# Halved input to a grouped convolution, smaller tap products, and expert products in the order of the sums

## The reference, cut to what matters

```python
# 1. deformable convolution block on the group-normalised input (here one channel per group)
xn = gn(x)
x_proj = xn @ w_in + b_in
x1 = gelu(layernorm(depthwise_conv3x3(xn) + dw_b) * ln_g + ln_b)
offset = x1 @ w_off + b_off                      # 8 groups x 9 taps x 2
mask = softmax(x1 @ w_msk + b_msk over 9 taps)
out = sum over 9 taps of mask * bilinear_sample(pad(x_proj), position + tap + offset)
x = x + out @ w_out + b_out
# 2. attention over the 256 tokens of each image
t = x as tokens; n = layernorm(t)
t = t + softmax(n @ n.T) @ n
# 3. mixture of 8 experts, top 2
n = layernorm(t)
p = softmax(n @ router_w + router_b); top 2, renormalised
t = t + sum over the two chosen experts of p * (n @ expert_w[e] + expert_b[e])
```

## Time and profile before

| | |
|---|---|
| Median of 3 runs | 83.26 us (83.23 to 83.63) |
| Profiled execution, its own time | 83.83 us |
| Its span, first to last instruction | 82.1 us |
| TensorE busy, weight load busy | 70.6 us (86%), 58.5 us (71%) |
| VectorE, ScalarE, GpSimd busy | 54.7 us (67%), 42.8 us (52%), 48.4 us (59%) |
| Mean granted TensorE clock | 0.964 |

### The profile page before, as it was taken

The page is one execution under the profiler, slowest core; times in us unless marked ns, Lnnn a source line. Parts: engine busy times, 40 slices in busy tenths (PEclk is TensorE's granted clock), DMA queues, the critical chain, the costliest instruction groups (busy, mean ns, idle before and its releaser), DMA issues.

```text
span 82.1 us, 1760 instructions
## 1 busy us (share of the span) xinstructions
PE 70.6 (86%) x655; PEld 58.5 (71%) x655; DVE 54.7 (67%) x103; ACT 42.8 (52%) x141; POOL 48.4 (59%) x78
## 2 busy tenths in 40 slices
PE   1999999999599999899799999997797989999600
PEld 1989879867399988698799989775444767666200
DVE  1141530363996899999997996646235758999950
ACT  0353200499669256969994000365993430299910
POOL 5107089998599699999999997000003500248920
PEclk9999999999999999999999999999999999999555
DMA  0412182004870000000000000000000000000014
GB/s 0 131 43 57 26 168 28 10 8 140 241 198 0 8 4 0 0 0 4 0 0 8 4 0 0 0 0 8 0 0 0 0 0 8 0 0 0 0 33 95
DMA packets 5607, 2.51 MB, mean 31 GB/s; under 512 B 4623, under 2 KB 5135, under 8 KB 5599
## 3 DMA queue, kind: packets, MB, share of 16 engines
q1 hardware_dynamic: 4895, 2.14, 10.8%
q10 hardware_dynamic: 704, 0.26, 1.2%
HBM read 0.95 MB, written 0.26 MB: 15 GB/s over the span
## 4 chain that ended last, share of the span: by engine, by line
PE 26%; DVE 25%; ACT 5%; issue 3%; POOL 2%; POOLq 1%; DVEq 0%
PE ps L654 10%; DVE prod L313 6%; DVE image_all L1144 6%; DVE image_all L1346 4%; PE ps L643 4%; PE ps L775 3%; ACT image_all L1002 3%; POOL image_all L529 2%; PE ps L785 2%; PE ps L793 2%; PE ps L756 1%; DVE prod L1367 1%; PE ps L694 1%; PE ps L718 1%; PE ps L702 1%
## 5 line engine op out<-in xcount | busy, mean ns | idle before, releaser
L538 PE MATMUL ps<-wide_ident 128*128 128x128 f32 x104 | 15.8, 309 | 1.8 <-POOL wide_ident L396 1.8
L538 PEld LDWEIGHTS ps<-wide_ident 128*128 128x128 f32 x104 | 14.3, 218 | 3.2 <-POOL wide_ident L396 1.8
L1144 DVE TENSOR_TENSOR image_all<-ps,images 128x896 f32<-128x896 f32 (+4 forms) x8 | 13.2, 1690 | 0.4 <-PE ps L643 0.4
L654 PE MATMUL ps<-wide_ident,image_all 128*128 128x128 f32 (+2 forms) x92 | 11.2, 275 | 0.9 <-DVE image_all L1144 0.9
L654 PEld LDWEIGHTS ps<-wide_ident,image_all 128*128 128x128 f32 (+2 forms) x92 | 10.0, 139 | 1.6 <-DVE image_all L1144 1.6
L643 PE MATMUL ps<-wide_ident,prod 128*128 128x128 f32 x81 | 9.9, 275 | 0.1
L520 POOL TENSOR_TENSOR prod<-prod,tok 128x256 f32<-128x256 f32 x2 | 1.9, 962 | 12.9 <-DVE prod L1296 12.9
L643 PEld LDWEIGHTS ps<-wide_ident,prod 128*128 128x128 f32 x81 | 8.8, 141 | 0.8 <-DVE prod L313 0.6
L309 POOL TENSOR_TENSOR my<-prob,hat 128x384 f32<-128x384 f32 x8 | 7.9, 1012 | 0.7 <-DVE ps L309 0.7
L313 POOL TENSOR_TENSOR prod<-my,hat 128x1152 f32<-128x1152 f32 x3 | 8.0, 2652 | 0.2
L313 DVE TENSOR_TENSOR prod<-ps,hat 128x1152 f32<-128x1152 f32 x6 | 7.9, 1350 | 0.1
(11 more groups left out here) (199 smaller groups left out, 143.9 us busy)
## 6 DMA issues: line engine op xcount, KB each, us to landing
images<-images SPq DMA_DIRECT2D x2, 300.0 KB, 4.2
images<-images SPq DMA_DIRECT2D x2, 280.0 KB, 3.6
x_tok<-in_x SPq DMA_DIRECT2D x4, 64.0 KB, 3.6
x_rows<-in_x SPq DMA_DIRECT2D x1, 128.0 KB, 2.8
x_rows<-in_x ACTq DMA_DIRECT2D x1, 128.0 KB, 3.2
expert<-in_expert_w SPq DMA_DIRECT2D x4, 32.0 KB
out_dram<-prod SPq DMA_DIRECT2D x2, 64.0 KB, 2.2
out_dram<-prod ACTq DMA_DIRECT2D x2, 64.0 KB, 2.5
```

Of the source, the lines that this page charges most:

```text
L538: pe.matmul(pbank(bank, P), ident, ident, start=True, stop=True)
L654: ins = pe.matmul(ps[0:last, SAMPLED, c * NJ:(c + 1) * NJ], taps[:, ty % SLOTS, tx, c, 0:last], ident, start=(ty == 0 and tx == 0 and c == ...
L1144: v.tensor_tensor(taps[:, ty % SLOTS, t0:t1, :, y0 * NI:y1 * NI], bcast(coef_rows(ty, t0, t1).rearrange("p (t j) -> p t j", j=P)[:, :, y0 ...
```

## The change

1. `PIECES`: the products of row 0 come in three pieces (0,2), (2,4), (4,5) in place of two, those of row 1 in two, (0,2), (2,5), in place of one.
2. `xnT` is written in two halves, and each convolution block waits for its half; the one warm matmul ahead of the convolution is left out.
3. GpSimd's constants (L452 to L467) are moved behind the pair sums (L510).
4. ScalarE makes a copy of the expert weights with the expert innermost, in the space of `x_rows`; TensorE uses it for images 2 and 6 (and waits for it ahead of all expert products), so that VectorE multiplies and sums these with the expert innermost.
5. VectorE multiplies image 5 before it sums image 2, not after.

```diff
@@ -46,7 +46,7 @@
 PAIRS_OF_ROW = (((0, 0),), ((1, 0), (0, 1)), ((0, 2), (2, 0), (1, 1)), ((2, 1), (1, 2)), ((2, 2),))
-PIECES = (((0, 2), (2, 5)), ((0, 5),), ((0, 5),), ((0, 5),), ((0, 2), (2, 4), (4, 5)))
+PIECES = (((0, 2), (2, 4), (4, 5)), ((0, 2), (2, 5)), ((0, 5),), ((0, 5),), ((0, 2), (2, 4), (4, 5)))
 HALVES = 2
@@ -59,7 +59,7 @@
 
-WARM = {"start": 5, "group sums": 5, "squares": 4, "normalised": 1, "hats": 30, "layer norm": 2,
+WARM = {"start": 5, "group sums": 5, "squares": 4, "hats": 30, "layer norm": 2,
         "projection weights": 2,
@@ -167,6 +167,7 @@
         row_f = sb("row_f", [P, 1])
+        expert_by_channel = x_rows[:, 0:NE * C].rearrange("p (c e) -> p c e", e=NE)
         image_all = sb("image_all", [P, H, W * C])
@@ -279,6 +280,7 @@
         VECTOR_GATED = (0, 1, 2, 4, 5, 6)
+        BY_CHANNEL = (2, 6)
         POOL_SUMS = ((0, 0, 2), (1, 0, 2))
@@ -449,22 +451,6 @@
                             ALU.mult).then_inc(late_ready, 1)
-            then(g.memset(tile_mask[:, :], 1.0))
-            then(where(tile_mask[:, :], [[-NE, GT]], 0, 1, ALU.is_ge, 0.0))
-            then(where(tile_mask[:, :], [[NE, GT]], NE - 1, -1, ALU.is_ge, 0.0))
-            g.tensor_tensor(expert_b_bd[:, :, :], bcast(expert_b8[:, :], 1, GT),
-                            bcast(tile_mask[:, :], 2, C), ALU.mult).then_inc(late_ready, 1)
-            g.iota(priority[:, :], [[-1, NE]], base=NE, channel_multiplier=0,
-                   allow_small_or_imprecise_dtypes=True)
-
-            g.iota(coord_x[:, :].rearrange("p (i j x) -> p i j x", i=K, j=K),
-                   [[1, K], [0, K], [1, W]], base=-1, channel_multiplier=0,
-                   allow_small_or_imprecise_dtypes=True)
-            g.iota(coord_ky[:, :], [[0, K], [1, K]], base=-1, channel_multiplier=0,
-                   allow_small_or_imprecise_dtypes=True)
-            g.iota(part_no[:, :], [[0, 1]], base=0, channel_multiplier=1)
-            g.iota(pixel_no[:, :], [[1, W]], base=0, channel_multiplier=0,
-                   allow_small_or_imprecise_dtypes=True).then_inc(late_ready, 1)
 
@@ -508,6 +494,23 @@
                 g.tensor_tensor(pair, pair, taps[:, PAIRED % SLOTS, tx + 1, :, 0:last], ALU.add).then_inc(taps_paired, 1)
+
+            then(g.memset(tile_mask[:, :], 1.0))
+            then(where(tile_mask[:, :], [[-NE, GT]], 0, 1, ALU.is_ge, 0.0))
+            then(where(tile_mask[:, :], [[NE, GT]], NE - 1, -1, ALU.is_ge, 0.0))
+            g.tensor_tensor(expert_b_bd[:, :, :], bcast(expert_b8[:, :], 1, GT),
+                            bcast(tile_mask[:, :], 2, C), ALU.mult).then_inc(late_ready, 1)
+            g.iota(priority[:, :], [[-1, NE]], base=NE, channel_multiplier=0,
+                   allow_small_or_imprecise_dtypes=True)
+
+            g.iota(coord_x[:, :].rearrange("p (i j x) -> p i j x", i=K, j=K),
+                   [[1, K], [0, K], [1, W]], base=-1, channel_multiplier=0,
+                   allow_small_or_imprecise_dtypes=True)
+            g.iota(coord_ky[:, :], [[0, K], [1, K]], base=-1, channel_multiplier=0,
+                   allow_small_or_imprecise_dtypes=True)
+            g.iota(part_no[:, :], [[0, 1]], base=0, channel_multiplier=1)
+            g.iota(pixel_no[:, :], [[1, W]], base=0, channel_multiplier=0,
+                   allow_small_or_imprecise_dtypes=True).then_inc(late_ready, 1)
 
@@ -565,11 +568,10 @@
                       skip_group_check=True)
-            keep_warm(7, WARM["normalised"])
             pe.wait_ge(conv_w_ready, 1)
             pe.wait_ge(consts, 3)
-            pe.wait_ge(x_normed, 1)
             for b in range(4):
+                pe.wait_ge(x_normed, 1 + b // 2)
                 lo, hi = (1, 6) if b == 0 else (0, 5) if b == 3 else (0, 6)
@@ -826,7 +828,7 @@
                     ins = pe.matmul(pbank(EXPERT[n], NE * C, h * NE * C), ln2T[q * C:(q + 1) * C, ga, h, :],
-                                    expert4[q * C:(q + 1) * C, :, :], start=True, stop=True)
+                                    (expert_by_channel if n in BY_CHANNEL else expert4)[q * C:(q + 1) * C, :, :], start=True, stop=True)
                 ins.then_inc(experts_done, 1)
@@ -846,6 +848,7 @@
             router(1)
+            pe.wait_ge(expert_turned, 1)
             for n in EXPERT_ORDER[:3]:
@@ -969,6 +972,8 @@
                 ins.then_inc(x_ctok_ready, 1)
+            act.wait_ge(late_in, 8 * 16)
+            act.activation(expert_by_channel[:, :, :], expert4[:, :, :].rearrange("p e c -> p c e"), ACT.Copy).then_inc(expert_turned, 1)
 
@@ -1099,8 +1104,10 @@
             v.wait_ge(gn_rstd_ready, 1)
-            v.tensor_tensor(xnT[:, :, 1:1 + H, :], xc,
-                            gn_rstd[:, :].unsqueeze(1).unsqueeze(1).to_broadcast([P, 4, H, NI]), ALU.mult).then_inc(x_normed, 1)
+            for half in range(2):
+                b = slice(2 * half, 2 * half + 2)
+                v.tensor_tensor(xnT[:, b, 1:1 + H, :], xc[:, b],
+                                gn_rstd[:, :].unsqueeze(1).unsqueeze(1).to_broadcast([P, 2, H, NI]), ALU.mult).then_inc(x_normed, 1)
 
@@ -1343,8 +1350,12 @@
                 v.wait_ge(experts_done, EXPERT_ORDER.index(n) + 1)
-                v.tensor_tensor(gated[:, ga, q, :, :, :], pbank(EXPERT[n]).rearrange("p (h e c) -> p h e c", h=HALVES, e=NE),
-                                bcast(by_image[:, q, :, :], 3, C), ALU.mult).then_inc(gated_ready, 1)
+                if n in BY_CHANNEL:
+                    v.tensor_tensor(gated_by_channel(ga, q, q + 1), pbank(EXPERT[n]).rearrange("p (h c e) -> p h c e", h=HALVES, e=NE),
+                                    bcast(by_image[:, q, :, :], 2, C), ALU.mult).then_inc(gated_ready, 1)
+                else:
+                    v.tensor_tensor(gated[:, ga, q, :, :, :], pbank(EXPERT[n]).rearrange("p (h e c) -> p h e c", h=HALVES, e=NE),
+                                    bcast(by_image[:, q, :, :], 3, C), ALU.mult).then_inc(gated_ready, 1)
 
@@ -1358,20 +1369,18 @@
                 ga, q = n // GI, n % GI
-                by_channel = gated[:, ga, q, :, :, :].rearrange("p h e c -> p h c e")
                 if n in ACT_GATED:
                     v.wait_ge(act_gated, ACT_GATED.index(n) + 1)
-                    by_channel = gated_by_channel(ga, q, q + 1)
                 else:
                     v.wait_ge(gated_ready, VECTOR_GATED.index(n) + 1)
-                v.tensor_reduce(moe[:, ga, q, :, :], by_channel, AX, ALU.add).then_inc(vector_summed, 1)
+                v.tensor_reduce(moe[:, ga, q, :, :], gated_by_channel(ga, q, q + 1), AX, ALU.add).then_inc(vector_summed, 1)
 
             gated_experts(4)
+            gated_experts(5)
             sum_experts(2)
-            gated_experts(5)
             sum_experts(3)
```

More of the change, by code:

```diff
@@ L241, in hybrid_block @@
         (tap_cols_ready, vec_cols_ready, ln_cols_ready, gn_rstd_ready, conv_squared, conv_rstd_ready, x_proj_ready, lower_ready, gT_ready, probs_ready, abs_ready,
-         my_ready, over_ready, x_mean_ready, x_ctok_ready, sampT_ready, sqT_ready, rT_ready, exp_done, attT_ready, ln2T_ready,
+         my_ready, over_ready, x_mean_ready, x_ctok_ready, expert_turned, sampT_ready, sqT_ready, rT_ready, exp_done, attT_ready, ln2T_ready,
          tok2_squared, tok2_rstd_ready, gap_exp, gateT_ready, act_gated, result_ready) = (
             sem(n) for n in ("tap_cols_ready", "vec_cols_ready", "ln_cols_ready", "gn_rstd_ready", "conv_squared", "conv_rstd_ready", "x_proj_ready", "lower_ready",
-                             "gT_ready", "probs_ready", "abs_ready", "my_ready", "over_ready", "x_mean_ready", "x_ctok_ready", "sampT_ready",
+                             "gT_ready", "probs_ready", "abs_ready", "my_ready", "over_ready", "x_mean_ready", "x_ctok_ready", "expert_turned", "sampT_ready",
                              "sqT_ready", "rT_ready", "exp_done", "attT_ready", "ln2T_ready",
```

## The result

| | before | changed |
|---|---|---|
| Median | 83.12 us (15 runs, 82.67 to 83.64) | 82.23 us (15 runs, 81.95 to 84.5) |
| Ratio | | 0.989, 95% interval 0.9862 to 0.9918 |
| Profiled execution, span | 83.83 us, 82.1 us | 81.98 us, 80.2 us |

The forecast was 82.5 us (82.1 to 83.1) and a ratio of 0.9913.

A forecast was written before the change was run, and what follows sets the result against it. No engine was taken to bound the whole; savings count only where others wait. Front 0.27, constants 0, pieces 0.26 and tail 0.20 sum to 0.73 us off 83.83, ratio 0.9913; on the median 83.26 that gives 82.5 us (82.1 to 83.1).

The forecast's parts named there:

- the pieces: Sampling stage, tap products of rows 0 and 1 in smaller pieces: 0.26 us gained, bounds 0 and 0.41.
- Front: Ahead of conv: halved normalised input, no warm matmul; conv starts at 10.89 in place of 11.16, 0.27 us gained.
- Constants: GpSimd's mask, priority and coordinates, 2.0 us, only fill a wait for ScalarE's magnitudes; moving them gains and costs zero.
- 43.49 + 0.14: Sampling stage: when VectorE, 0.14 us late from two extra pieces, would be free for row 3's product, 43.63.
- the step that row 3's product sets the stage: Sampling stage: VectorE's product of row 3, released by TensorE, starts 0.26 us earlier and that gain lasts.
- rival (a): Sampling stage: GpSimd's third weights set the rest, TensorE's row 4 gaps stay; gain 0.47, 82.8 us; chance 0.15.
- TensorE's gaps in row 4: Sampling stage: TensorE's waits for VectorE in row 4, 0.41 us left, taken to cover the 0.26 gain.
- The rule on the pipe's drain and the fixed part: VectorE pieces: next operation waits for an empty pipe, fixed part 0.16 us; gain would be 0.10, not 0.26.
- Tail: End of kernel: adjacent expert sums save 0.36 us twice, but ScalarE's last gated expert limits the gain to 0.20.
- My list of VectorE's times: Tail: VectorE's products and sums timed one by one from 71.88 us, with sum 6 ending at 77.35.
- Rival (c): Conv: without the warm matmul the TensorE clock falls to half; up to +2.5 us, 85.0 us; chance 0.05.
- My argument against it: Ahead of conv: TensorE would idle only 0.14 us, and held its clock with 0.76 us idle on its loads.

## Why the prediction was right, and where its steps were not

- **The total:** the forecast of 0.73 us stands against 0.82 in distances. Two of its three terms came out as worked out. The third, the pieces, was too low by 0.08 and rested on a step that failed, so that the total came so near is in part luck. Of the 0.3 us between 82.5 and the measured 82.23, another 0.14 come from the start, 83.26 us as the median of 3 runs, where that of 15 was 83.12.
- **Front, 0.27 us:** right to the hundredth, but I counted the missing warm matmul among its reasons, as standing in the way of the half. It doesn't: 0.55 us with it. The whole gain is the halves'.
- **Constants, 0:** right in the execution that tested it. GpSimd's idle time ahead of the add at 61.19 shrank by 2.4 us to 9.65. That ahead of the hats grew only from 0.93 to 1.74, not by the 2 us of the constants, as the hats came 1.29 us earlier in that execution.
- **Pieces, 0.26 forecast, 0.34 measured:** two sizes and one mechanism were off. A piece costs 0.06 or 0.07. VectorE was free for row 3's product sooner than "43.49 + 0.14": I took the recorded end of the instruction before as the moment at which the next can start, but in the changed kernel the product starts at 42.25 while the flag's instruction is recorded from 42.18 for 0.14. So it started 0.35 us earlier in the stage (16.64 us after the first y-weights, 16.99 before) and not 0.26. And the step that row 3's product sets the stage failed. From before and after alone it would have passed, 0.35 and 0.34 being so near; but with a piece less on VectorE the product started another 0.07 earlier and the stage gained nothing. What ends the stage is what rival (a) named, GpSimd's third weights and TensorE's unbroken 52 transposes behind them: the weights' loads start 16.87 us after the first y-weights in the kernel before, 16.88 in the changed one and 16.87 with row 0 unsplit. They cap the gain at TensorE's gaps in row 4, which I put at 0.41 from the recorded idle times and which were worth 0.34: 48.61 + 2.15 - 44.71 = 6.05 us for the 52 in the kernel before (their first load began at 44.71), 5.71 now. Rival (a) had the bound right and its effect wrong: it left the gaps open. No run makes GpSimd's weights earlier, so that they are the limit is read from these rows.
- **The rule on the pipe's drain and the fixed part** (the Trainium skill, VectorE: DVE Perf Modes, "The DRAIN you can't avoid" and "The TRN2 errata"), by which the two pieces would cost an estimated 0.31 us: as a price of splitting the trace disagrees, the two cost 0.06 and 0.07 (2.71 for 2.65, 2.61 for 2.54). The section on the drain itself adds that a next operation that is not held starts earlier, and that is what these rows show.
- **Tail, 0.20 forecast, 0.21 measured:** right, through the mechanism named: 0.36 us saved on each sum, and only the part up to ScalarE's end counts. ScalarE's copy took 0.67 us, not 0.4, inside its idle time. The order, which I put into the same sum, brings nothing with adjacent sums. My list of VectorE's times left out its wait for TensorE ahead of product 5, 0.12 us.
- **Rival (c), the clock at conv, chance 0.05:** it happened, in 6 of 57 executions without the warm matmul. The fall was as named, its price was not: conv grew by 1.68 us, not by 2.5, as the clock was back before conv ended (from conv's first load to the first y-weights both profiles have 17.43 us for 15.76). The rest of the 2.3 us is, as far as the two show, that they also reached the full pace late at the start (normalising at 10.11 and 10.17). My argument against it, that the array had kept the clock over 0.76 us without loads, was weak: in the kernel before the warm matmul ended that very gap, and without it the loads idle 0.97 us. The Trainium skill (TensorE: Matmul & The Clock Gate, "What's actually happening") has throttling as the default that activity releases; the traces agree in direction, as the clock was at 0.50 in conv only where a matmul ahead of it was missing, and in two of eight such profiles.

## What to carry to other kernels

Splitting a product so that its consumer can start pays only where the consumer's wait for it is on the path, and it pays up to the next engine's limit: here the same edit was worth 0.34 us in row 1 and nothing in row 0. When summing a stage, take the distance between starts, not recorded ends, and look for a run of work that would be unbroken once the gap is gone: its length is the cap. A matmul that only keeps the array busy can be free on the path and still matter in some executions; its removal is not judged by a median.

## What the runs showed of the hardware

- The moment at which the array reaches full pace differs between executions of one program, and here it moves everything behind it: ten identity matmuls at 5.3 us took 1.47 to 2.50 us in fourteen profiled executions (eight at full pace take 1.14), and the normalising began at 9.31 to 10.35, later where they took longer, though not strictly in step (1.47 and 1.49 us go with 9.31 and 9.52). That is a microsecond of spread in a single profile, more than the change is worth. The granted clock reads 1.00 in all fourteen from the start, even while ten such matmuls take 2.50 us at 1.8 us, so the start of a profile is read from the pace.
- Both profiled executions with the clock at half in conv were ones in which that full pace came late (2.41 and 2.47 us), and without the warm matmul. The other six without it had 1.47 to 2.08 and kept the clock; one with it came as late (2.50, the kernel before) and kept it too. The times fit that in part: the changed kernel's three near 84.5 lie within 0.03 us of each other, where its others spread over 1.0 us, as if all three had begun equally late. But its run of 82.98 us, 1.00 above the profiled one, looks as late by its time and didn't fall. Two profiles don't make a rule.
- A VectorE sum over 8 elements of fp32 with a step of 32 elements took 1.03 us for 512 elements, with adjacent elements 0.67.
